# Graph layer and mixture of experts on one core: the sum that the scatters add to is written ahead of them, shared rows follow tile by tile, one-hot columns are spread to 16 bits, and the products of a 96-slot position run in another order

## What is computed

```python
def gnn(h, src, dst):
    agg = segment_sum(h[src], dst, 625)
    h = relu(batch_norm(((1 + eps) * h + agg) @ W1 + b1))   # 512 -> 1024
    ...
    return h_in + relu(batch_norm(h @ W2 + b2))             # 1024 -> 512

def ffn(h):
    shared = sum(silu(h @ sWg[e]) * (h @ sWu[e]) @ sWd[e] for e in range(2))
    gate = top 6 of softmax(h @ Wr), made to sum to 1
    routed = sum(gate[:, e] * (silu(h @ Wg[e]) * (h @ Wu[e]) @ Wd[e]) for e in range(64))
    return shared + routed + h

x = x + gnn(layernorm(x), src, dst)
x = x + ffn(layernorm(x))
```

## Time and profile before

| | us |
|---|---|
| median of 3 runs | 781.27 (780.87 to 785.67) |
| the profiled execution, its own time | 782.4 |
| its span, from the first to the last instruction | 780.7 |
| PE busy in the span | 722.4 |
| DVE, ACT and POOL busy | 260.5, 195.1 and 174.7 |

### The profile page before, as it was taken

One profiled execution on the slowest core, in us unless ns is written; L12 is line 12 of the kernel. 1 busy time (PEld: TensorE's weight loads), 2 busy tenths in 40 slices (PEclk: granted clock), 3 DMA queues, 4 the chain that ended last, 5 costly groups with the idle time before them and its releaser, 6 DMA issues. The chain is left out here.

```text
span 780.7 us, 17521 instructions
## 1 busy us (share of the span) xinstructions
PE 722.4 (93%) x7096; PEld 478.5 (61%) x7096; DVE 260.5 (33%) x788; ACT 195.1 (25%) x497; POOL 174.7 (22%) x157
## 2 busy tenths in 40 slices
PE   2699999879999999999999999999999999489993
PEld 2597776556666666555566666655566666356662
DVE  7983524975221442222221212121233222012100
ACT  1222321402332222211222222121222333033331
POOL 4000000011222232232332222222333332123211
PEclk9999999999999999999999999999999999789996
DMA  9970021426999999999999999999999999999921
GB/s 265 407 280 3 0 108 62 166 75 222 354 341 337 347 387 382 392 392 380 385 387 390 378 401 377 384 394 389 383 384 372 373 374 368 342 369 364 337 36 23
DMA packets 57265, 236.35 MB, mean 303 GB/s; under 512 B 6171, under 2 KB 6335, under 8 KB 40286
## 3 DMA queue, kind: packets, MB, share of 16 engines
q1 hardware_dynamic: 46004, 211.33, 70.8%
q0 software_dynamic: 10144, 20.56, 11.4%
q10 hardware_dynamic: 1034, 3.30, 1.1%
HBM read 222.32 MB, written 12.83 MB: 301 GB/s over the span
## 5 line engine op out<-in xcount | busy, mean ns | idle before, releaser
L424 POOL DMA_INDIRECT xg<-x_tab,idx_sb x64 | 71.8, 1121 | 387.9 <-DVE idx_sb L942 220.0
L1368 PE MATMUL ps<-ring,xT 128*64 128x256 f32 x1296 | 156.5, 383 | 0.6 <-ACT xT L608 0.6
L439 POOL DMA_INDIRECT out<-ysb,idx_sb x64 | 92.5, 1445 | 202.4 <-DMA out<-ysb,idx_sb 124.4
L1368 PEld LDWEIGHTS ps<-ring,xT 128*64 128x64 f32 x1296 | 88.1, 137 | 43.8 <-issue 3.4
L628 ACT ACTIVATE ysb<-ps 64x256 f32<-64x256 f32 x64 | 24.2, 377 | 332.3 <-PE ps L1368 152.5
L935 DVE TENSOR_REDUCE gates<-ps 128x1 f32<-128x3 f32 (+1 forms) x62 | 10.0, 162 | 267.7 <-PE ps L1275 267.0
L1368 PE MATMUL ps<-ring,hTj 128*64 128x256 f32 x624 | 75.5, 384 | 0.0
L1368 PE MATMUL ps<-w,xT 128*64 128x256 f32 x608 | 75.1, 390 | 0.0
L903 DVE TENSOR_TENSOR onehot<-iotaAB,slotv 125x640 bf16<-125x640 f32 (+1 forms) x64 | 67.3, 1051 | 2.6 <-PE ps L1283 1.8
L999 DVE SCALAR_TENSOR_TENSOR hs<-hs,gates,ps 128x256 f32<-128x256 f32 x64 | 30.7, 480 | 90.2 <-PE ps L1373 43.8
L1368 PEld LDWEIGHTS ps<-ring,hTj 128*64 128x64 f32 x624 | 42.1, 136 | 30.1 <-issue 11.9
(11 more groups left out here) (237 smaller groups left out, 818.2 us busy)
## 6 DMA issues: line engine op xcount, KB each, us to landing
ring<-in_L_ffn_Wg SPq DMA_DIRECT2D x41, 1024.0 KB, 20.7
ring<-in_L_ffn_Wu SPq DMA_DIRECT2D x40, 1024.0 KB, 21.2
ring<-in_L_ffn_Wd SPq DMA_DIRECT2D x39, 1024.0 KB, 22.5
w<-in_L_ffn_Wd SPq DMA_DIRECT2D x20, 1024.0 KB, 22.4
w<-in_L_ffn_Wg SPq DMA_DIRECT2D x19, 1024.0 KB, 21.6
w<-in_L_ffn_Wu SPq DMA_DIRECT2D x19, 1024.0 KB, 21.3
ring_x<-in_L_ffn_Wu SPq DMA_DIRECT2D x5, 1024.0 KB, 20.2
ring_x<-in_L_ffn_Wd SPq DMA_DIRECT2D x5, 1024.0 KB, 20.3
```

Source lines behind the costliest of these rows:

```text
L424: g.indirect_dma_start(out=xg[j % NX][0:ROWS[j], :], out_offset=None, in_=x_tab, in_offset=bass.IndirectOffsetOnAxis(ap=idx_sb[0:ROWS[j], ...
L439: g.indirect_dma_start(out=out, out_offset=bass.IndirectOffsetOnAxis(ap=idx_sb[0:ROWS[j], j:j + 1].bitcast(u32), axis=0), in_=ysb[h][0:ROW ...
L1368: last = t_.matmul(ps[h * BIG:(h + 1) * BIG, bank, 0:AW], big(k), w[:, k, h * AW:(h + 1) * AW], start=(k == 0), stop=(k == KD - 1))
```

## The change

It has five parts.

1. `out` is no longer filled with zeros. SyncE writes `x_sb` (the layer's input plus its residual) to it with two plain DMAs, ahead of the 14th weight load. Scatter 0 waits for that.
2. The shared experts' outcome is collected in `x_sb` by itself: the first shared expert's tiles are copied there, the second's added. After the scatters of positions 41, 45, 49, 53 and 57 one tile of 125 rows is added to `out` with two accumulating DMAs (`add_shared`), and the scatter that follows each waits for them.
3. `iota_m` becomes a whole 125 x 625 tile, and ScalarE spreads each group's column to a 16-bit 125 x 625 tile `rep` (`spread`), of which there are ten; `one_m` compares the two. Weight buffer `ring7` shares its place with six of the ten and its first load waits for the last comparison.
4. The aggregation of the last block comes behind the branch of the further rounds, and VectorE adds it to `hT` from PSUM in place of ScalarE's copy.
5. In 96-slot positions but position 0, TensorE runs the 64-column products of gate and up, then the 32-column products of gate and up, and only then the transposes. Down products of 96-slot positions run the 32-column products first.

```diff
-    BASE_AFTER = 50
+    SHARED_AFTER = [41, 45, 49, 53, 57]
+    NREP = 10
...
+                if i == 7:
+                    sp.wait_ge(s_sm, NG)
...
+                if i == 13:
+                    for a, b in PARTS:
+                        sp.dma_start(out.rearrange("(t p) d -> p t d", p=P)[a:b, :, :], x_sb[a:b, :, :]).then_inc(s_base0, 16)
...
-            g.iota(iota_m[:], pattern=[[1000, T], [1, G]], base=1000, channel_multiplier=0).then_inc(s_cst, 1)
+            g.iota(iota_m[:], pattern=[[0, U], [1000, T], [1, G]], base=1000, channel_multiplier=0).then_inc(s_cst, 1)
...
-                if j == BASE_AFTER + 1:
-                    pool.wait_ge(s_base, 32)
+                if j == 0:
+                    pool.wait_ge(s_base0, 32)
+                if j - 1 in SHARED_AFTER:
+                    pool.wait_ge(s_base, 32 * (SHARED_AFTER.index(j - 1) + 1))
...
-            def add_base():
-
-                pool.wait_ge(s_sy, NS * T)
-                pool.wait_ge(s_scat[0], (BASE_AFTER + 2) // 2 * 16)
-                pool.wait_ge(s_scat[1], (BASE_AFTER + 1) // 2 * 16)
+            def add_shared(t, j):
+
+                pool.wait_ge(s_sy, (NS - 1) * T + t + 1)
+                pool.wait_ge(s_scat[0], (j + 2) // 2 * 16)
+                pool.wait_ge(s_scat[1], (j + 1) // 2 * 16)
                 for a, b in PARTS:
-                    g.dma_start(out.rearrange("(t p) d -> p t d", p=P)[a:b, :, :], x_sb[a:b, :, :],
-                                accum_op=ALU.add).then_inc(s_base, 16)
+                    g.dma_start(out[t * P + a:t * P + b, :], x_sb[a:b, t, :], accum_op=ALU.add).then_inc(s_base, 16)
...
+            def spread(b):
+                for g in range(b * GB, (b + 1) * GB):
+                    if g >= NREP:
+                        act.wait_ge(s_sm, g - NREP + 1)
+                    sc.activation(rep[g % NREP][:], col_m[:, g * U:(g + 1) * U].unsqueeze(2).broadcast_to([P, U, P]),
+                                  ACT.Copy).then_inc(s_rep, 1)
...
+                if spread:
+                    last = v.tensor_tensor(one_m[slot][:], iota_m[:], rep[g % NREP][:], ALU.is_equal)
...
+            v.tensor_tensor(block, block, ps[:, 4 + (T - 1) % 2, 0:KD * P].rearrange("p (k n) -> p k n", k=KD),
+                            ALU.add).then_inc(s_hT, 1)
...
+            def tiled(bank, big, small, w, done):
+
                 if small is not None:
...
+                    small_tiles(bank, small, w)
+                big_tiles(bank, big, w).then_inc(done, 1)
+
+            def gate_and_up(x, w_gate, w_up, j):
+                big_tiles(0, lambda k: x[:, k, 0:BIG], w_gate())
+                if j >= 1:
+                    pe.wait_ge(s_mul, j)
+                big_tiles(1, lambda k: x[:, k, 0:BIG], w_up())
+                small_tiles(0, lambda k: x[:, k, BIG:CAP], w_gate()).then_inc(s_g, 1)
+                small_tiles(1, lambda k: x[:, k, BIG:CAP], w_up()).then_inc(s_u, 1)
```

143 lines of the change are left out of this document (83 added, 60 removed).

## The result

The changed kernel takes 796.18 us (median of four runs, 792.54 to 796.96) against 782.43 us for the kernel before, run beside it: a ratio of 1.0158 with an interval of 1.0117 to 1.0199, so 9 to 16 us slower; the medians differ by 13.8. The forecast was 784.4 us with a range of 765 to 799. The time lies in that wide range, but outside the likeliest case's own range of 776 to 792, and nearer to rival 1 (801.6) than to the forecast. The profiled execution is the fastest of the four, at 792.54 us, with a span of 790.8 us.

The account below looks back on a forecast made before the run. TensorE, busy 722 of 781 us, and the nearly as full chain of scatters were taken as the bounds. The terms +13.3 - 5.2 - 1.5 - 3.5 gave +3.1 us on 781.27, so 784.4 us, range 765 to 799.

Parts of the forecast that it names:

- the likeliest case: The forecast itself, 784.4 us, chance 0.42, with its own range of 776 to 792 us.
- rival 1: GpSimd's queue behind scatters 41 to 57: all pairs cost their full load, 10.4 us each; 801.6 us, chance 0.25.
- the tail: End of the stretch to scatter 58: weights have landed, the chain catches up at 3.9 us a scatter, -5.2 us.
- The term for the pairs: Five pairs in the scatter chain: 10.4 us delay for each of the first two, 8.0 for the three later.
- The mis-sized term: Scatters 41 to 58 without the pairs: 155.3 us, less 1.1 us for each of nine scatters behind position 49.
- From position 41 on the chain sets the pace: Late positions: back-to-back scatters, not TensorE, set the time; scatters 41 to 58 take 190.1 us against 176.85, +13.3.
- The order of products: TensorE's 96-slot positions: net 0.3 us saved each, counted only in positions 1 to 5, -1.5 us; bounds 0 and 9.5.
- The aggregation: Front of the kernel: faster 16-bit comparison, 0.3 us a group; last aggregation ends at 58.5 instead of 62.05, -3.5 us.
- Base written first: Writing `x_sb` to `out` instead of GpSimd's zeros: taken as 0 us, bounds 0 and 3.
- Rival 3: The stall goes as a whole, the slack hiding all five pairs: 753 us, chance 0.05.
- rival 4: VectorE's comparison gets no faster: 784.4 + 4.4 = 789 us, chance 0.04.
- Rival 2: Pairs in the scatter chain are short, 2.5 us for 229 KB by the skill's rule: 767 us, chance 0.24.

Follow-up runs that it names:

- the kernel without pairs: The changed kernel without any of the five pairs of adds, shared experts' rows left out of the output: 769.65 us, ratio 0.9847.
- the kernels with the pairs late: The changed kernel with its pairs behind scatters 57, 58, 59, 60 and 61: 788.38 us; the same with the old order of products: 789.13 us.
- the kernel with the late fills: One add behind scatter 50 and a third output buffer, with GpSimd's two table fills issued behind VectorE's edge codes: 772.46 us, ratio 0.9840.

## Why the prediction was right, and where it was off

**The mechanism** was right: pairs stand in a chain of scatters that has no room, and TensorE stops behind them. Shown by the kernel without pairs. The size was not: +3.1 us were forecast, within what the forecast itself called no change, and +13.8 came. By stretches of the profiled execution, the front was forecast at -5.0 and gave -4.5, scatters 41 to 58 at +13.3 and gave +20.2, the tail at -5.2 and gave -5.6. That the total fell in the range of 765 to 799 owes much to the width of that range.

**The term for the pairs** was right too: 2 x 10.4 + 3 x 8.0 = 44.8 us were forecast. The five pairs held the chain for 45.8 us, less 0.3 each for the hand-over that any scatter has: 44.3. That the sum agrees so well is partly luck: the pairs behind 49 and 53 cost 9.8 and 9.6 us where 8.0 was taken, and the last one 5.2.

**The mis-sized term** is what the rest of the stretch takes, "155.3" less "1.1 us off each of the nine scatters": 145.3 us. It took 197.07 - 44.3 = 152.8. (The 155.3 itself should be 154.4: six of the scatters 41 to 57 are of 64 slots and eleven of 96.) The scatters were in fact relieved more than that. For one stretch the DMA engines moved 108 GB/s where it is 370 under load, and two scatters landed in 4.2 and 4.3 us (tile `ysb`, 676 to 695 us, and the busy times of 680 to 690).

```profile
DMA to landing us min/median/max: 4.2/4.3/4.3
```

```profile
680.00:690.00 10.00, 8.01 (x72) 5.23 (x74) 0.74 (x2) 3.99 (x13) 3.75 (x3) 0.62 0.57 108
```

But the chain could not use it. The step that failed is "From position 41 on the chain sets the pace". After a stop TensorE sets it: scatter 53 was issued 7.8 us and scatter 57 4.8 us after the landing of the one before, where 0.9 is usual, both behind a gather in GpSimd's queue whose index came late. Without these two waits, 6.9 and 3.9 us over the usual, the stretch would have taken 142.0 us, less than the forecast's 145.3. Here are TensorE's products after the stop ahead of scatter 53, and the slot product on which that gather waits:

```profile
681.99 1.94 PE L1407 MATMUL ps<-ring,hTj 128*32 128x128 f32 x32 [9.46 <-ACT hTj L643]
683.85 3.68 PE L1400 MATMUL ps<-ring,hTj 128*64 128x256 f32 x16
...
693.61 0.40 PE L1308 MATMUL ps<-gsel,onehot 125*128 125x5 bf16 x10
```

Two sentences of the forecast fell with it. "Scatters already stand later than that, so no cost" was said of the slot product, which the new order puts behind the up product: in a steady stretch it holds, behind a stop it does not. And the clock, "hidden while the chain sets the pace": the first 32 and 16 products after the stop took 1.94 and 3.68 us where they take 1.08 and 1.95, 2.6 us on the path to that index. The granted clock of the stretch is 0.62, so a part of it ran at 1.2 GHz. How much of the 7.8 us belongs to each was not tried by itself. Nor was the late gather taken away in any run: that it cost these 10.8 us is read from the timeline.

**The tail**, -5.2 forecast, was -5.6.

**The order of products**, -1.5 forecast over positions 1 to 5. The first copies of `y` of positions 0 and 4 stand at

```profile
188.10 0.38 ACT L649 ACTIVATE ysb<-ps 64x256 f32<-64x256 f32 x1 [3.28 <-PE ps L1400]
...
225.70 0.38 ACT L649 ACTIVATE ysb<-ps 64x256 f32<-64x256 f32 x1 [2.82 <-PE ps L1400]
```

or 9.40 us a position, as forecast, against 38.62 / 4 = 9.66 before (191.25 to 229.87): -0.26 each, -1.3 in five. That the late positions are worth nothing fits the kernels with the pairs late: what TensorE gains there, the scatters lose.

**The aggregation**, -3.5 forecast. The comparison is as fast as hoped, and a group takes 1.11 us of VectorE instead of 1.44. But the first aggregation starts at 29.95 us and not at 29.1, since VectorE lost 1.6 us to the fills (with them out of the way it starts at 28.38); and the last, forecast to end at 58.5, ends here:

```profile
29.95 5.83 PE L1151 MATMUL ps<-aT,h 125*128 125x125 f32 x40 [0.17 <-issue]
...
55.36 4.70 PE L1151 MATMUL ps<-aT,h 125*128 125x125 f32 x40 [1.67 <-issue]
```

at 60.06. That is -2.0 against 62.05, and even this is a lucky execution: in the kernels tried with the same front the last one starts between 55.9 and 57.0 us, because the first aggregation takes up to 7.4 us instead of 5.83. The first `y` copy of position 0 tells the same: 188.10 us here, 190.3 to 193.0 in the nine other kernels with this front and order, 191.25 in the kernel before and 192.64 in it with the third buffer. There is also a gap of 1.5 to 1.9 us ahead of the last one that the forecast did not have, where TensorE now takes the branch on further rounds. This was read from the traces and not tested.

**Base written first**: 0 forecast, and this was not so at the front. "The zeros are issued by GpSimd in the first microseconds, where nobody waits for it" overlooked that they kept GpSimd's fills away from VectorE until 7.25 us; without them VectorE loses the 1.6 us above, as the kernel with the late fills shows. What the write of `x_sb` itself costs was not tried.

**The forecast's own tests.** "TensorE stops at least four times" and the 18 to 20 us between the scatters around a pair came true. The forecast would also be wrong "if the stops cost over 25 us in all", and by that test it was: they are 27.2 without the one at the end.

**Rivals.** Rival 1, the full load each, came half true: the next scatter comes 9.8 and 9.6 us behind the pairs of 49 and 53, but 5.2 behind that of 57. The measured 796.18 lies beyond its halfway mark of 793. Rival 3 has fallen with the stops of TensorE, rival 4 with the comparison's 0.48 us. Rival 2, the short pair by the Trainium skill's rule (DMA: Bandwidth & Descriptors, "Anatomy of one DMA"), is excluded under load: 2.5 us by the rule for its larger DMA, and the DMAs of the first four pairs land 5.1 to 9.5 us after their issue. Once the loads have ended they land in 3.6 to 3.8, still more than the rule.

## What to carry to other kernels

Before a transfer is cut into pieces, find out what the smallest of its kind costs where it will stand: beside saturated loads an add had a fixed 8.5 us here and only 2.3 for each 256 KB, so that five pieces held the chain for 45.8 us where one held it for 19.65. When two resources are both within a few per cent of the bound, such as TensorE at 9.4 and the scatters at 9.6 to 9.8 us a position, an improvement of one can be eaten by the other, and what helped here is room between them: one more buffer brought 6.6 to 9.0 us in all three kernels that got it. And a queue that issues in order must be read as one chain, with the gathers in it and what they wait for.

## What the runs showed of the hardware

- A VectorE operation with one input waited while GpSimd filled a table: 1.80 us, against 0.31 in the kernel before, where the fills come later, and 0.22 once the fills were moved. The Trainium skill (SBUF — State Buffer, "SBUF: two separate sides") describes a pair of ports shared by VectorE and GpSimd, which the one that starts first holds for a whole instruction. The trace agrees as to the wait. It also shows the operation waiting through both fills, up to 6.66 us, and not only through the one that had begun. The kernel before shows a second case: its cast of `srcf`, begun at 3.57 beside GpSimd's fill of `zrows` (3.50 to 4.11), took 0.62 us, and 0.21 in the changed kernel, which has no such fill.
- The comparison with 16-bit operands throughout takes 0.48 us for 625 numbers in each partition instead of 0.81 with an fp32 column:

```profile
12.02 0.48 DVE L728 TENSOR_TENSOR one_m<-iota_m,rep 125x625 bf16<-125x625 int16 x1
```

  Counted from start to start it is 0.39 us instead of 0.72, a gain of 0.33. The rule of the Trainium skill (VectorE: DVE Perf Modes, "Mode 2×_1P") on 16-bit operands, from which the forecast had 0.3 to 0.36, holds here.

- A gather issued right behind a 1.28 MB add from the same engine lands 17.6 us later, where one before the add takes 6.7 to 8.5. In the kernel before it is 17.5, and behind a single tile of 256 KB 8.7.
